# SyncE asks by a table of tiles when it may load an expert's weights, in place of a fixed distance of four tiles

## The chip, the cores and the metric

The kernel runs on one core of a Trainium2 chip. The metric is the device time of the whole program in microseconds (us), one launch, lower is better. The core's engines are TensorE (PE; its weight loads are listed as PEld), VectorE (DVE), ScalarE (ACT), GpSimd (POOL) and SyncE (SP), which computes nothing and issues DMAs. Each runs its own list of instructions in order, and they wait for each other by semaphores. A name with a "q" behind it (SPq) is the part of an engine that reads registers, branches, waits and issues.

## The reference

Two blocks on x of 8 x 256 tokens with 256 features, each an attention and a feed-forward part, all with residual additions:

```
x = x + attention0(layernorm(x), ctx, ctx)              # 16 heads, no projections
x = x + moe(layernorm(x), gate_w, w_gate, w_up, w_down) # 64 experts, top 8, F = 192
x = x + attention1(layernorm(x), ctx, Wq, Wk, Wv, Wo)   # causal
x = x + block_sparse_ffn(layernorm(x), ...)             # 16 blocks of 64, top 4
```

The change lies in moe. Each of the 2048 tokens chooses 8 of 64 experts; with g = rows of an expert times w_gate, u = rows times w_up, the expert's output is (silu(g) * u) times w_down, and a token's 8 outputs are summed with the weights of the choice:

```
topk_w, topk_ids = top_k(softmax(x @ gate_w.T), 8);  topk_w /= topk_w.sum()
g = ragged_dot(sorted_tokens, w_gate.T, group_sizes)
u = ragged_dot(sorted_tokens, w_up.T, group_sizes)
out = ragged_dot(silu(g) * u, w_down.T, group_sizes)
```

## The kernel before, in words

Stages run one behind the other: constants and preparation; attention 0, with the routing of the experts (class Route) worked into it; the expert tiles (`experts`); attention 1, with the gathering of the experts' outputs worked into it; and the last feed-forward part with the output projection.

Route writes, for each expert, a list of its tokens to DRAM (POOL, L835: 128 indirect DMAs) and then makes the tables of tiles on DVE (`make_tables`). A tile is 128 entries of one expert's list, so an expert has as many tiles as its list needs, and an expert's tiles follow each other. `k.table` has one column per tile and three rows: the expert, the buffer (the expert's number among those that have tiles, modulo WRING = 4), and 1 where the tile is its expert's first. `make_tables` computes them with the tile number on the partitions (`below`, `sums`, two halves a of 128 tiles), PE turns them onto one partition (`turned`), and DVE copies them (`line`, `line_i`). POOL meanwhile finishes the lists and gathers the tokens of each tile (`ids_raw`, L841), which DVE then converts (L1011).

`experts(nc, k, begin, end)` is called twice, for tiles 0 to 159 and for tiles 160 to 191; the second call does its work only if more than 160 tiles are in use (`needed`). In the profiled execution the lines of the stage have run for 160 tiles. Tiles are taken in rounds of R = 8, round 0 written out with constants and the others in a loop. For tile t:

- SP (`step` under `block.sync`, L1136 to L1145) reads three entries of the table into registers (`value_load`; L1136 expert, L1137 buffer, L1138 first or not), waits until `down_ready` has reached t - WRING + 1, that is until the down product of tile t - 4 is done, and issues two DMAs, w_gu (384 KB) and w_down (192 KB), each with the condition `fresh`. If the tile isn't its expert's first, no data moves and only the semaphore `w_in[j]` is raised.
- POOL gathers the 128 token rows of the tile by an indirect DMA (L1157, L1159), up to eight tiles ahead.
- PE turns the rows (L1172), multiplies them by w_gu (L1181, after it has waited for `w_in[j]`), turns the gated hidden rows of the tile before (L1191) and multiplies those by w_down (L1199), which raises `down_ready`.
- ACT copies the turned rows (L1247) and applies silu (L1253), and issues the store of the results (L1258). DVE multiplies by u (L1288), copies the turned hidden rows (L1294) and weighs the result (L1302).

`down_ready` counts down products. SP's wait for it keeps a load from overwriting a buffer that is still read; since the four buffers go around by expert and not by tile, four tiles back is sufficient for that whatever the sizes of the experts.

Of the kernel before, what the change touches and what calls it, by code (L numbers as in the profile page):

```python
# [7 lines left out]
F32 = mybir.dt.float32  # L8
BF16 = mybir.dt.bfloat16
I32 = mybir.dt.int32  # L10
ALU = mybir.AluOpType
ACT = mybir.ActivationFunctionType
AX = mybir.AxisListType

P = 128
# [21 lines left out]
START = 6  # L37
LISTS = EXPERTS * TILES
WRING = 4
IN_FLIGHT = 4  # L40

BLOCKS, TOP_B, HID = 16, 4, 1024
# [659 lines left out]
class Route:  # L702
# [8 lines left out]
    def open(self, nc, k, ctx, sem, ps):  # L711
        sb = lambda n, shape, dt: ctx.enter_context(nc.sbuf_tensor(f"rt_{n}", shape, dt))
        E = EXPERTS
        self.nc, self.k, self.ps = nc, k, ps
        self.gate = sb("gate", [P, DC, E], F32)
        self.before = sb("before", [P, P], BF16)
        self.ones = sb("ones", [P, P], BF16)
        self.list_end = sb("list_end", [P, E], F32)
        self.token = sb("token", [P, TILES], I32)
        self.tile_no = sb("tile_no", [P, 2], F32)  # L720
        self.zeros = sb("zeros", [P, LISTS], I32)
        self.stats = sb("stats", [P, 2, 6], F32)
        self.moments = sb("moments", [P, 2, 2], F32)
        self.rstd = sb("rstd", [P, 2], I32)
        self.newton = sb("newton", [P, 2], F32)
        self.rows = sb("rows", [P, 2, 2, D + E], F32)
        self.xn_t = sb("xn_t", [P, DC * SEQ], F32)
        self.logits = sb("logits", [P, 2, E], F32)
        self.others = sb("others", [P, 2, E], F32)
        self.best = sb("best", [P, 2, 8], F32)  # L730
        self.expo = sb("expo", [P, 2, E], F32)
        self.chosen = sb("chosen", [P, 2, E], F32)
        self.total = sb("total", [P, 3, 2], F32)
        self.mask = sb("mask", [P, TILES, E], BF16)
        self.earlier = sb("earlier", [P, TILES + 1, E], BF16)
        self.back = sb("back", [P, 2, E], F32)
        self.now = sb("now", [P, 2, E], F32)
        self.place = sb("place", [P, TILES, E], F32)
        self.top = sb("top", [P, 2, TOP_K], F32)
        self.idx = sb("idx", [P, TILES, TOP_K], I32)  # L740

        self.shift_g = sb("shift_g", [P, E], F32)
        self.place_g = sb("place_g", [P, TILES, E], F32)
        self.top_g = sb("top_g", [P, TILES, TOP_K], F32)
        self.count = sb("count", [P, 6, E], F32)
        self.count_i = sb("count_i", [P, E], I32)
        self.below = sb("below", [P, 2, 3, E], F32)
        self.sums = sb("sums", [P, 2, 4], F32)
        self.distinct = sb("distinct", [P, 1], F32)
        self.row = sb("row", [P, 2], F32)  # L750
        self.row_i = sb("row_i", [P, 2], I32)
        self.ids_raw = sb("ids_raw", [P, 2, P], I32)
        self.ids_f = sb("ids_f", [P, 2, P], F32)
        self.line = sb("line", [1, 3, ETABLE], F32)
        self.line_i = sb("line_i", [1, ETABLE], I32)

        self.c_in, self.zero_set, self.zeroed = sem("constants_in"), sem("zero_set"), sem("lists_zeroed")
        self.outs_zeroed = sem("outs_zeroed")
        self.own, self.none_set = sem("route_own"), sem("none_set")
        self.xn_ready, self.xn_turned, self.xn_copied, self.logits_ready = sem("xn_ready"), sem("xn_turned"), sem("xn_copied"), sem("logits_ready")  # L760
        self.shifted, self.exped, self.counted, self.ranked = sem("shifted"), sem("route_exped"), sem("counted"), sem("ranked")
        self.ranks_read, self.weights_ready, self.slots_ready = sem("ranks_read"), sem("weights_ready"), sem("slots_ready")
        self.rows_out = [sem("rows_out0"), sem("rows_out1")]
        self.scattered, self.ids_in = [k.indirect(f"scattered{q}") for q in range(IN_FLIGHT)], k.indirect("ids_in")
        self.tables, self.counts_ready = sem("tables_own"), sem("counts_ready")
        self.rows_ready, self.ids_f_ready, self.turned = sem("rows_ready"), sem("ids_f_ready"), sem("turned")
        self.constants = [(self.gate, "gate"), (self.before, "c_before"), (self.ones, "c_ones"), (self.list_end, "c_list_end"),
                          (self.token, "c_token"), (self.tile_no, "c_tile")]
# [184 lines left out]
    def make_tables(self, dve):  # L953
# [20 lines left out]
        then(nc.vector.tensor_copy(k.tiles_used[:], ends[0:1, E - 1:E]))  # L974
        then(nc.vector.tensor_scalar(some, tiles, 0.5, None, ALU.is_gt))
        then(nc.vector.tensor_reduce(distinct[:], some, AX.X, ALU.add))
        then(nc.vector.tensor_scalar(distinct[:], distinct[:], -1.0, None, ALU.add))

        for a in range(2):
            then(nc.vector.tensor_scalar(below[:, a, 0, :], ends, self.tile_no[:, a:a + 1], None, ALU.is_le))  # L980
            then(nc.vector.tensor_tensor(below[:, a, 1, :], below[:, a, 0, :], some, ALU.mult))
            then(nc.vector.tensor_tensor(below[:, a, 2, :], below[:, a, 0, :], tiles, ALU.mult))
            then(nc.vector.tensor_reduce(sums[:, a, 0:3], below[:, a], AX.X, ALU.add))
            then(nc.vector.tensor_scalar(sums[:, a, 0:1], sums[:, a, 0:1], float(E - 1), None, ALU.min))
            then(nc.vector.tensor_tensor(sums[:, a, 1:2], sums[:, a, 1:2], distinct[:], ALU.min))
            then(nc.vector.tensor_tensor(sums[:, a, 3:4], self.tile_no[:, a:a + 1], sums[:, a, 2:3], ALU.subtract))
            then(nc.vector.tensor_scalar(sums[:, a, 3:4], sums[:, a, 3:4], float(TILES - 1), None, ALU.min))
            then(nc.vector.tensor_scalar(self.row[:, a:a + 1], sums[:, a, 0:1], float(TILES), None, ALU.mult))
            nc.vector.tensor_tensor(self.row_i[:, a:a + 1], self.row[:, a:a + 1], sums[:, a, 3:4], ALU.add).then_inc(self.rows_ready, 1)

# [9 lines left out]

        dve.wait_ge(self.turned, 1)
        then(nc.vector.tensor_copy(line[:, 0:2, :].rearrange("p q n -> p (q n)"), self.ps[0:1, :]))
        then(nc.vector.memset(line[:, 2, 0:1], 1.0))
        then(nc.vector.tensor_tensor(line[:, 2, 1:ETABLE], line[:, 1, 1:ETABLE], line[:, 1, 0:ETABLE - 1], ALU.not_equal))
        then(nc.vector.tensor_copy(k.table[:, 0, :], line[:, 0, :]))
        then(nc.vector.tensor_copy(self.line_i[:], line[:, 1, :]))
        then(nc.vector.tensor_scalar(k.table[:, 1, :], self.line_i[:], WRING - 1, None, ALU.bitwise_and))
        then(nc.vector.tensor_copy(k.table[:, 2, :], line[:, 2, :]))
        dve.wait_ge(self.ids_in, 32)  # L1010
        nc.vector.tensor_copy(self.ids_f[:], self.ids_raw[:]).then_inc(self.ids_f_ready, 1)  # L1011
# [69 lines left out]
def experts(nc, k, begin, end):  # L1081
# [7 lines left out]
    with ExitStack() as ctx:  # L1089
# [32 lines left out]
        with nc.Block() as block:  # L1122
# [10 lines left out]
            def _(sp):  # L1133
                def step(i, j):
# [4 lines left out]

                    fresh = None if isinstance(i, int) and t == 0 else other > 0  # L1140

                    wait(sp, down_ready, t - WRING + 1)
                    sp.dma_start(w_gu[:, bass.ds(ring, 1)].rearrange("p a c n -> p (a c n)"),
                                 k.dram["w_gu"][bass.ds(expert, 1)].rearrange("e p c n -> (e p) (c n)"), cond=fresh).then_inc(w_in[j], 16)
                    sp.dma_start(w_down[:, bass.ds(ring, 1)].rearrange("p a c n -> p (a c n)"),  # L1145
# [20 lines left out]
            def _(pe):  # L1166
# [62 lines left out]
                        rings = step(i, j, rings, first=(isinstance(i, int) and i == j == 0), left=R - j if last else R)  # L1229

                with needed(pe):
                    turn_rows(0, 0)
                    turn_rows(0, 1)
                    steps(0)
                    with pe.Fori(1, ROUNDS - 1) as i:
                        steps(i)
                    steps(ROUNDS - 1, last=True)
                    turn_hidden(ROUNDS - 1, R - 1)
                    down(ROUNDS - 1, R - 1, buffer_of(ROUNDS - 1, R - 1))
# [43 lines left out]
            def _(dve):  # L1283
# [6 lines left out]
                def copy_hidden(i, j):  # L1290
                    t = R * i + j
                    dve.wait_ge(hidden_turned, t + 1)
                    wait(dve, down_ready, t - 1)
                    nc.vector.tensor_copy(hidden_t[:, j % 2], ps[0:FH, 4 + j % 2, 0:2 * P]).then_inc(hidden_copied, 1)  # L1294

                def weigh(i, j):
                    t = R * i + j
                    expert = dve.value_load(table[0:1, 0, bass.ds(t, 1)], min_val=0, max_val=EXPERTS - 1)
                    dve.wait_ge(down_ready, t + 1)
                    if not isinstance(i, int) or i:  # L1300
                        dve.wait_ge(out_done[j], 16 * i)
                    nc.vector.tensor_scalar(result[:, j], ps[:, 6 + j % 2, 0:D], rows[:, j, bass.ds(expert + D, 1)], None, ALU.mult).then_inc(result_ready, 1)  # L1302
# [542 lines left out]
def build(nc, dram, out):  # L1845
# [11 lines left out]
    with ExitStack() as ctx:  # L1857
# [2 lines left out]
        k.kst = sb("stacked_keys", [ROWS + MROWS, 4, HSTEP, SEQ], BF16)  # L1860
        k.ao = sb("attention_out", [P, TILES, D], F32)
        k.slot = sb("slot", [P, TILES, TOP_K], I32)
        k.table = sb("tile_table", [1, 3, ETABLE], I32)
        k.tiles_used = sb("tiles_used", [1, 1], I32)
        k.ids = sb("slot_tokens", [P, ETABLE], I32)

# [75 lines left out]
```

## Time and the profile before

| | us |
|---|---|
| median of 3 runs | 1505.9 |
| lowest and highest | 1501.64, 4754.02 |
| profiled execution, its time | 1501.42 |
| its span, first to last instruction | 1499.6 |

The mean granted TensorE clock was 0.826 of full speed in that execution. Over the whole span PE was busy for 67% and the other engines less: DVE 41%, POOL 32%, ACT 24%.
### The profile page before, as it was taken

How to read it: one execution, taken by the hardware profiler on the slowest of the kernel's cores; microseconds unless marked ns; L12 is line 12 of the kernel's file. 1: busy time of each engine (PE TensorE's matmuls, PEld its weight loads, DVE VectorE, ACT ScalarE, POOL GpSimd, SP SyncE). 2: the span in 40 equal slices, each digit the busy share in tenths (PEclk: the TensorE clock that was granted, in tenths of full speed). 3: DMA queues.
4: the chain of work that ended last, by engine and by line, in shares of the span. 5: the costliest groups of instructions: out<-in, count | busy, mean ns of one | idle time of the engine just before them, and what ended most of it. 6: DMA issues, size and time to landing. Idle time of an engine off the chain costs nothing. (4 is left out here: it accounts for less than half of the span.)

```text
span 1499.6 us, 26078 instructions
## 1 busy us (share of the span) xinstructions
PE 1007.6 (67%) x5671; PEld 650.4 (43%) x5672; DVE 617.9 (41%) x1846; ACT 361.8 (24%) x884; POOL 483.5 (32%) x641
## 2 busy tenths in 40 slices
PE   5476757640078778888888878601445658859999
PEld 4333434320045555555555555401224436636665
DVE  5467665652023333333333333322535657423220
ACT  4534343410011111111111111110023334512221
POOL 4401334455543333333333333077453320000000
PEclk9868686655589999999999999855567779969999
DMA  6766664100055454445545655235543333210000
GB/s 195 255 172 158 74 74 66 28 18 0 4 154 159 141 165 150 150 150 151 158 147 165 176 164 157 86 98 139 139 112 109 101 99 92 52 69 11 15 14 18
DMA packets 102128, 164.36 MB, mean 110 GB/s; under 512 B 20352, under 2 KB 70400, under 8 KB 101808
## 3 DMA queue, kind: packets, MB, share of 16 engines
q1 hardware_dynamic: 61040, 99.39, 24.4%
q0 software_dynamic: 17984, 43.21, 10.8%
q10 hardware_dynamic: 23040, 20.98, 4.2%
q8 instruction: 30, 0.49, 0.2%
q14 instruction: 34, 0.28, 0.1%
HBM read 174.72 MB, written 45.15 MB: 147 GB/s over the span
## 5 line engine op out<-in xcount | busy, mean ns | idle before, releaser
L1181 PE MATMUL ex_ps<-ex_w_gu,ex_rows_t 128*128 x640 | 278.5, 518 | 89.8 <-DMA ex_w_down<-in_w_down_dram 70.8
L1159 POOL DMA_INDIRECT ex_rows<-moe_rows,ex_idx x160 | 155.5, 972 | 129.1 <-POOL ex_idx L1157 117.7
L835 POOL DMA_INDIRECT expert_lists<-rt_token,rt_idx x128 | 124.4, 972 | 203.9 <-DMA expert_lists<-rt_token,rt_idx 110.4
L647 ACT ACTIVATE a_probs<-a_ps 128x512 f32<-128x512 f32 (+1 forms) x256 | 133.8, 540 | 206.3 <-remote 67.1
L1199 PE MATMUL ex_ps<-ex_w_down,ex_hidden_t 96*128 x640 | 169.6, 388 | 1.0 <-DVE ex_hidden_t L1294 1.0
L492 PE MATMUL a_ps<-stacked_keys,a_qst 96*128 96x256 bf16 (+1 forms) x512 | 119.6, 307 | 73.8 <-DMA stacked_keys<-k_stack 30.4
L1181 PEld LDWEIGHTS ex_ps<-ex_w_gu,ex_rows_t 128*128 128x128 f32 x640 | 108.4, 198 | 121.7 <-issue 116.4
L509 PE MATMUL a_ps<-a_qst,stacked_keys 98*128 98x256 bf16 (+1 forms) x512 | 116.5, 301 | 65.9 <-issue 30.3
L1253 ACT ACTIVATE ex_act_g<-ex_ps 128x192 f32<-128x192 f32 x160 | 52.8, 330 | 440.2 <-PE ex_ps L1181 412.3
L1391 POOL DMA_INDIRECT cb_gathered<-expert_outs,cb_idx x128 | 122.1, 954 | 45.0 <-issue 40.9
L1294 DVE COPY ex_hidden_t<-ex_ps 96x256 f32<-96x256 f32 x160 | 67.3, 420 | 142.7 <-PE ex_ps L1191 126.2
L1302 DVE TENSOR_SCALAR ex_result<-ex_ps,ex_rows 128x256 f32<-128x256 f32 x160 | 77.4, 484 | 96.0 <-PE ex_ps L1199 85.8
L1199 PEld LDWEIGHTS ex_ps<-ex_w_down,ex_hidden_t 96*128 96x128 f32 x640 | 110.9, 194 | 12.4 <-issue 2.3
L588 DVE TENSOR_REDUCE a_negmax<-a_ps 128x2 f32<-128x512 f32 x128 | 85.8, 688 | 63.4 <-PE a_ps L492 52.1
L585 DVE TENSOR_REDUCE a_blockmax<-a_ps 128x3 f32<-128x384 f32 x128 | 70.2, 554 | 96.7 <-remote 49.2
L1288 DVE TENSOR_TENSOR ex_hidden<-ex_act_g,ex_ps 128x192 f32<-128x192 f32 x160 | 56.7, 354 | 115.0 <-ACT ex_act_g L1253 110.9
L1157 POOL COPY ex_idx<-slot_tokens 128x1 int32 (+1 forms) x160 | 29.3, 183 | 224.6 <-DVE ex_result L1302 216.7
L492 PEld LDWEIGHTS a_ps<-stacked_keys,a_qst 96*128 96x128 bf16 x512 | 51.2, 112 | 115.9 <-issue 43.3
L509 PEld LDWEIGHTS a_ps<-a_qst,stacked_keys 98*128 98x128 bf16 x512 | 54.0, 111 | 96.0 <-issue 54.8
L1649 POOL TENSOR_TENSOR x<-x,ff_b 128x256 f32 x16 | 11.5, 747 | 226.0 <-DVE ff_xn L1805 226.0
L1247 ACT COPY ex_rows_t<-ex_ps 128x256 f32<-128x256 f32 x160 | 58.8, 368 | 92.8 <-PE ex_ps L1172 91.5
L532 PE MATMUL a_ps<-a_probs,a_v_aug 128*32 128x256 f32 (+1 forms) x1024 | 79.4, 439 | 0.0
(200 smaller groups left out, 1405.0 us busy)
## 6 DMA issues: line engine op xcount, KB each, us to landing
ex_w_gu<-in_w_gu_dram SPq DMA_DIRECT2D x160, 384.0 KB
ex_w_down<-in_w_down_dram SPq DMA_DIRECT2D x160, 192.0 KB
expert_outs<-ex_result ACTq DMA_DIRECT2D x160, 128.0 KB
k_stack<-split_parts SPq DMA_DIRECT2D x16, 384.0 KB, 2.6
a_qst<-q_stack SPq DMA_DIRECT2D x32, 192.0 KB
stacked_keys<-k_stack SPq DMA_DIRECT2D x32, 192.0 KB
a_qst<-q_stack SPq DMA_DIRECT2D x32, 128.0 KB
stacked_keys<-k_stack SPq DMA_DIRECT2D x32, 128.0 KB
```

The lines of the kernel that those rows point to most:

```text
L492: last = pe.matmul(bank[:, at:at + keys], qst[0:ROWS, u, s, j * P:(j + 1) * P], kst[0:ROWS, u, s, 0:keys], start=True, stop=True)
L509: last = pe.matmul(bank[:, at:at + SEQ - first], kst[:, u, s, j * P:(j + 1) * P], qst[:, u, s, first:SEQ], start=True, stop=True)
L532: last = pe.matmul(outs_dq[VW * r:VW * (r + 1), first:SEQ], v_aug[:, b_par, j, s, :], probs[:, 4 * g + r, j * SEQ:j * SEQ + SEQ - first], ...
L585: nc.vector.tensor_reduce(blockmax[:, u % 2, s, :], ps[:, QK_BANKS[s % 3], 0:cols].rearrange("p (b n) -> p b n", n=P), AX.X, ALU.max, nega ...
L588: nc.vector.tensor_reduce(negmax[:, u % 2, :, s], ps[:, QK_BANKS[s % 3], :].rearrange("p (j n) -> p j n", j=2), AX.X, ALU.max, negate=True ...
L647: nc.scalar.activation(probs[:, s, 0:cols], ps[:, 2 + s % 2, 0:cols], ACT.Exp, scale=scale).then_inc(exped, 1)
L835: nc.gpsimd.indirect_dma_start(k.lists, bass.IndirectOffsetOnAxis(ap=self.idx[:, t, s:s + 1], axis=0), self.token[:, t:t + 1], None).then_ ...
L1159: nc.gpsimd.indirect_dma_start(rows[:, j, :], None, k.xn.rearrange("t p d -> (t p) d"), bass.IndirectOffsetOnAxis(ap=idx[:, j:j + 1], axis ...
L1181: last = pe.matmul(ps[:, 2 + j % 2, 0:2 * FF], rows_t[:, j % 2, c * P:(c + 1) * P], w_gu[:, bass.ds(ring, 1), c, :].rearrange("p a n -> p ...
L1199: last = pe.matmul(ps[:, 6 + j % 2, 0:D], hidden_t[:, j % 2, c * P:(c + 1) * P], w_down[:, bass.ds(ring, 1), c, :].rearrange("p a n -> p ( ...
L1302: nc.vector.tensor_scalar(result[:, j], ps[:, 6 + j % 2, 0:D], rows[:, j, bass.ds(expert + D, 1)], None, ALU.mult).then_inc(result_ready, 1)
L1391: nc.gpsimd.indirect_dma_start(self.gathered[:, u, j, s, :], None, k.outs.rearrange("t p d -> (t p) d"), bass.IndirectOffsetOnAxis(ap=self ...
```

## The change

SP's wait takes its count from a fourth row of the table. For a tile of expert number d (among those with tiles) it holds the number of tiles of the experts up to number d - 4, the last user of the buffer, or the tile's number minus 7 if that is more (so that SP is at most eight tiles ahead, the number of the semaphores `w_in`), and one is added. PE raises `down_ready` by one at its start, so that the count is never zero, and DVE's waits for `down_ready` and the fixed distance of the second call are one higher. `make_tables` computes the new row: a running count of the experts with tiles (`kinds`), for each half four operations for the count and one that packs it with the expert's number into one value, and for the line an integer copy, a shift and a mask that take them apart.

```diff
+LOADS_AHEAD = 8
...
             then(nc.vector.tensor_reduce(distinct[:], some, AX.X, ALU.add))
+            then(nc.vector.tensor_tensor_scan(self.kinds[:], one, some, 0.0, ALU.mult, ALU.add))
...
         for a in range(2):
...
+            then(nc.vector.tensor_scalar(below[:, a, 3, :], self.kinds[:], float(WRING - 1), sums[:, a, 1:2], ALU.add, ALU.is_le))
+            then(nc.vector.tensor_tensor(below[:, a, 3, :], below[:, a, 3, :], tiles, ALU.mult))
+            then(nc.vector.tensor_reduce(sums[:, a, 4:5], below[:, a, 3, :], AX.X, ALU.add))
+            then(nc.vector.scalar_tensor_tensor(sums[:, a, 4:5], self.tile_no[:, a:a + 1], float(1 - LOADS_AHEAD), sums[:, a, 4:5], ALU.add, ALU.max))
+            then(nc.vector.tensor_scalar(sums[:, a, 0:1], sums[:, a, 0:1], 256.0, sums[:, a, 4:5], ALU.mult, ALU.add))
...
+        then(nc.vector.tensor_copy(self.line_i[:, 0, :], line[:, 0, :]))
...
-        then(nc.vector.tensor_copy(k.table[:, 0, :], line[:, 0, :]))
-        then(nc.vector.tensor_copy(self.line_i[:], line[:, 1, :]))
-        then(nc.vector.tensor_scalar(k.table[:, 1, :], self.line_i[:], WRING - 1, None, ALU.bitwise_and))
+        then(nc.vector.tensor_scalar(k.table[:, 0, :], self.line_i[:, 0, :], 8, None, ALU.logical_shift_right))
+        then(nc.vector.tensor_scalar(self.line_i[:, 0, :], self.line_i[:, 0, :], 255, None, ALU.bitwise_and))
+        then(nc.vector.tensor_scalar(k.table[:, 3, :], self.line_i[:, 0, :], 1.0, None, ALU.add))
+        then(nc.vector.tensor_copy(self.line_i[:, 1, :], line[:, 1, :]))
+        then(nc.vector.tensor_scalar(k.table[:, 1, :], self.line_i[:, 1, :], WRING - 1, None, ALU.bitwise_and))
...
                     fresh = None if isinstance(i, int) and t == 0 else other > 0
-                    wait(sp, down_ready, t - WRING + 1)
+                    if begin == 0:
+                        used = sp.value_load(table[0:1, 3, bass.ds(t, 1)], min_val=1, max_val=ETILES)
+                        sp.wait_ge(down_ready, used)
+                    else:
+                        wait(sp, down_ready, t - WRING + 2)
...
                 with needed(pe):
+                    pe.sem_inc(down_ready, 1)
...
-                    wait(dve, down_ready, t - 1)
+                    wait(dve, down_ready, t)
...
-                    dve.wait_ge(down_ready, t + 1)
+                    dve.wait_ge(down_ready, t + 2)
...
-        k.table = sb("tile_table", [1, 3, ETABLE], I32)
+        k.table = sb("tile_table", [1, 4, ETABLE], I32)
```

## Rows read from the trace of the kernel before

**Rows 1.** Windows by stage; the columns stand in the first line.

```profile
core 0: us, PE busy (x) PEld busy (x) DVE busy (x) ACT busy (x) POOL busy (x), PEclk, DMA share, GB/s
0.00:300.00 300.00, 195.07 (x1293) 114.04 (x1295) 182.23 (x579) 126.31 (x261) 100.11 (x98) 0.78 0.55 128
300.00:413.00 113.00, 20.17 (x107) 11.00 (x105) 27.98 (x131) 7.06 (x15) 61.50 (x64) 0.50 0.04 8
421.00:960.00 539.00, 449.19 (x1904) 297.56 (x1905) 199.08 (x475) 98.23 (x319) 180.46 (x313) 0.96 0.51 155
```

**Rows 2.** Waits of PE from 430 to 960: total us, times, longest.

```profile
PE ex_ps L1181 <- DMA ex_w_down<-in_w_down_dram: 70.8, 43, 3.4
PE ex_ps L1181 <- issue: 18.6, 18, 1.6
```

**Rows 3.** Waits of SP, the line of the loads.

```profile
SPq L1143 <- PE ex_ps L1199: 5.6, 9, 1.4
```

**Rows 4.** SP by source line: ns min/median/max, first and last start.

```profile
L1137 SPq TENSOR_LOAD <-tile_table x160: 5/267/520, 414.3 to 955.4; - x160
L1138 SPq TENSOR_LOAD <-tile_table x160: 3/263/524, 414.8 to 956.1; - x160
L1143 SPq DMA_DIRECT2D ex_w_gu<-in_w_gu_dram x160: 4/97/673, 415.6 to 957.0; - x160
L1145 SPq DMA_DIRECT2D ex_w_down<-in_w_down_dram x160: 5/93/549, 416.2 to 957.5; - x160
```

**Rows 5.** Timeline of PE, 429 to 435: the starts of three tiles.

```profile
429.61 0.81 PE L1181 MATMUL ex_ps<-ex_w_gu,ex_rows_t 128*128 x2
...
432.21 0.81 PE L1181 MATMUL ex_ps<-ex_w_gu,ex_rows_t 128*128 x2
...
434.81 0.81 PE L1181 MATMUL ex_ps<-ex_w_gu,ex_rows_t 128*128 x2
```

**Rows 6.** Timeline of PE, 465 to 475, and L1181 by source.

```profile
465.27 1.64 PE L1181 MATMUL ex_ps<-ex_w_gu,ex_rows_t 128*128 x2 [2.55 <-DMA ex_w_down<-in_w_down_dram]
...
469.47 0.81 PE L1181 MATMUL ex_ps<-ex_w_gu,ex_rows_t 128*128 x2
...
L1181 PE MATMUL ex_ps<-ex_w_gu,ex_rows_t x640: 484/488/1004, 421.4 to 960.4; 128*128 x160
```

**Rows 7.** SP by source line within 444 to 447 us, one tile.

```profile
L1136 SPq FUSED_REGOPS  x2: 51/110/169, 444.4 to 444.8; - x2
L1136 SPq TENSOR_LOAD <-tile_table x1: 275/275/275, 444.5 to 444.5; - x1
L1137 SPq FUSED_REGOPS  x2: 51/102/153, 445.0 to 445.4; - x2
L1137 SPq TENSOR_LOAD <-tile_table x1: 267/267/267, 445.1 to 445.1; - x1
L1137 SPq SEQ_ASSERT  x1: 18/18/18, 445.6 to 445.6; - x1
L1138 SPq FUSED_REGOPS  x2: 51/99/147, 445.7 to 446.1; - x2
L1138 SPq TENSOR_LOAD <-tile_table x1: 263/263/263, 445.8 to 445.8; - x1
L1138 SPq SEQ_ASSERT  x1: 16/16/16, 446.4 to 446.4; - x1
L1143 SPq FUSED_REGOPS  x2: 48/114/179, 446.5 to 446.7; - x2
```

**Rows 8.** SP's computed counts of the helper `wait`, L55.

```profile
L55 SPq ALU_OP  x57: 13/37/282, 439.5 to 940.7; - x57
```

**Rows 9.** Timeline ahead of the stage: POOL's gather of ids, DVE's conversion.

```profile
404.10 0.97 POOL L841 DMA_INDIRECT rt_ids_raw<-expert_lists,rt_row_i  x1 [3.62 <-DMA expert_lists<-rt_token,rt_idx]
405.38 0.96 POOL L841 DMA_INDIRECT rt_ids_raw<-expert_lists,rt_row_i  x1 [0.30 <-issue]
408.48 0.29 DVE L1011 CAST rt_ids_f<-rt_ids_raw 128x256 f32<-128x256 int32 x1 [62.08 <-DMA rt_ids_raw<-expert_lists,rt_row_i]
```

More of the change, by code:

```diff
@@ L746, in open @@
         self.count_i = sb("count_i", [P, E], I32)
-        self.below = sb("below", [P, 2, 3, E], F32)
-        self.sums = sb("sums", [P, 2, 4], F32)
+        self.below = sb("below", [P, 2, 4, E], F32)
+        self.sums = sb("sums", [P, 2, 5], F32)
         self.distinct = sb("distinct", [P, 1], F32)
@@ L754, in open @@
         self.line = sb("line", [1, 3, ETABLE], F32)
-        self.line_i = sb("line_i", [1, ETABLE], I32)
+        self.line_i = sb("line_i", [1, 2, ETABLE], I32)
+        self.kinds = sb("kinds", [P, E], F32)
         self.c_in, self.zero_set, self.zeroed = sem("constants_in"), sem("zero_set"), sem("lists_zeroed")
@@ L982, in make_tables @@
             then(nc.vector.tensor_tensor(below[:, a, 2, :], below[:, a, 0, :], tiles, ALU.mult))
-            then(nc.vector.tensor_reduce(sums[:, a, 0:3], below[:, a], AX.X, ALU.add))
+            then(nc.vector.tensor_reduce(sums[:, a, 0:3], below[:, a, 0:3], AX.X, ALU.add))
             then(nc.vector.tensor_scalar(sums[:, a, 0:1], sums[:, a, 0:1], float(E - 1), None, ALU.min))
```

## The prediction

> **What bounds the kernel now.** I began with the windows by stage [rows 1]. The change touches one stage, the expert tiles from 421 to 960 us: 539 of the 1499.6 us, at a granted TensorE clock of 0.96. No engine's column is full there (PE 449 of 539 us), so the next question is what PE waits for. The waits of PE [rows 2] say: 70.8 us in 43 waits for the landing of ex_w_down, and only 18.6 us at its own issue. Read by itself, this is a stage whose weights come too late, and loading them earlier looks like the cure.
>
> The other end of that wait must be read before that is believed: what kept SyncE from issuing earlier? The waits of SP [rows 3] answer it. At L1143 SP waited for the down products of PE (the wait that the change loosens) 5.6 us in total, nine times, at most 1.4 us. So in most of the 160 tiles the buffer was already free when SP came to ask. Outside those nine, SP isn't four tiles ahead; it is late by its own work. The sources of SP show that work [rows 4]: it issues the first w_gu load at 415.6 and the 160th at 957.0, that is 541.4 us for 159 steps, 3.41 us a tile. PE's own pace, where nothing holds it, is read from the starts of consecutive tiles [rows 5]: 429.61, 432.21, 434.81, which is 2.60 us a tile, or 416 us for 160. The stage lasts as long as SP's list of instructions and not as long as PE's, and PE's last w_gu product starts at 960.4, 3 us after SP's last issue [rows 4, 6].
>
> Where do 3.41 us go when the two DMA issues take 97 and 93 ns at the median [rows 4]? Each tile reads three entries of the table into registers, and each read is two FUSED_REGOPS, a TENSOR_LOAD of some 265 ns and a SEQ_ASSERT [rows 7]. In the step at 444 to 447 us the reads of L1136, L1137, L1138 begin at 444.4, 445.0 and 445.7 and the work of L1143 at 446.5 [rows 7]. Three reads are 2.1 of that step's time. The rows of SP list no idle time inside them.
>
> The Trainium skill, in "Perfetto Trace Analysis", section "What DMA-bound means", gives as the sign of a bound DMA issuer a sequencer track that is solid with DMA slices. Here that sign fails: the DMA slices are about a tenth of SP's step, and it is solid with register loads. By that sign SP would be passed over.
>
> **The change, part by part.**
>
> SP, new read (one per tile). Where the address is computed at run time, a read costs (445.7 - 444.4) / 2 = 0.65 us of SP's time [rows 7]; its parts 51 + 267 + 153 + 18 ns are 0.49, and the rest is the pause after each of four instructions. In round 0 the addresses are constants and there is no first FUSED_REGOPS; L1137 and L1138 begin at 414.3 and 414.8 [rows 4], so 0.55 by these rounded rows and the parts without the 51 ns. 152 x 0.65 + 8 x 0.55 = 103 us. Nothing lies beside it: SP runs its instructions one behind the other, and the new read stands ahead of the wait and of both loads. The bounds: 0.50 us, if every new read were as short as the first spacing, gives 80; 0.8 us, the longest spacing in rows 7 (445.7 to 446.5), gives 128. I take 0.65 because the reads of the loop are the like of the new one, and the third spacing holds a pause ahead of its SEQ_ASSERT (446.4) that the first two lack.
>
> SP, the computed count. `wait` computed t - 3 in an instruction of its own for three tiles of a round: 57 ALU_OPs of 37 ns [rows 8]. They go: 2 us, at most 4 with the pause behind them. The wait itself rides on the next instruction before and after, and I cost a register count as I do the computed one, at nothing; as a separate instruction of the ALU_OP's length it would be 160 x 0.04 = 6 us more, inside the bounds above.
>
> SP, the looser wait. It can give back no more than the 5.6 us that SP waited [rows 3]. Who gains from a lead of eight tiles? Only a queue that gets ahead. SP needs 3.41 now and about 4.0 then, PE 2.60, so SP will hardly reach the old limit of four, let alone eight. The new count is never stricter than the old one (a buffer's former expert ended at least four tiles back), so no new wait comes, and nothing is queued behind one. The rank of the loads, their bytes and their queue stay.
>
> PE, DVE inside the stage: one semaphore increment at the start, and counts one higher for DVE's waits. They concern work that is not late. Nothing.
>
> DVE, the tables: one scan, ten short operations for the two halves and three for the line, each behind a semaphore. DVE sits idle for 62.08 us before it may convert the ids at 408.48, since the ids come from POOL's scatters and gather [rows 9]. Fourteen operations with their waits at 1 us each (the conversion there takes 0.29) would be 14 us, under 62. Nothing on the path. Without that cover it would be those 14 us at most.
>
> PE must wait longer per tile for the weights, which is the place where the time shows: its waits grow by what SP's step grows. The clock is the second-order term. After a stall of 2.55 us PE ran its next tile at half speed, and that tile took 469.47 - 465.27 = 4.20 us [rows 6]. More stall means more of those. In stages where PE is busy 65% of the time the clock stood at 0.78 [rows 1]; after the change PE has 2.6 us of work in a step of 4.0, the same share. At 0.78, 44% of the tiles would take 4.20 and the others 2.60, a mean of 3.3, still under SP's 4.0. So the clock falls, and the end doesn't feel it.
>
> **The sum.** 103 (read) - 2 (ALU_OPs) - 6 (waits) = +95 us on SP's list and so on the stage. The profiled execution took 1501.42 us around a span of 1499.6; the middle one of the three runs is 1505.9 and the lowest 1501.64, so the profiled one stands at their low end. 1501.4 + 95 = 1596.4 us, +6.3% on that execution, +6.0% on 1505.9. Where the stall goes: PE waits some 95 us more for the loads, and the granted clock of the stage drops from 0.96 toward 0.8.
>
> **The rivals.**
>
> Faster (A). The loads land early and PE keeps its own pace. The stage is then 160 x 2.60 = 416 in place of 539 us: 1501 - 123 = 1378. For it: the 70.8 us in rows 2. It decides if SP in truth waited for buffers for most of its time, which [rows 3] deny with 5.6 us, or if a read of the table costs SP nothing. The rule behind it is in the Trainium skill, "DMA: Bandwidth & Descriptors", "Rules for kernel authors": issue a DMA early and wait for it late, so that its fixed cost overlaps. The rule would want it; the trace shows that this issuer has no earlier time to issue at.
>
> Not slower (B). The fourth read overlaps the third, so that it adds at most 0.2 us: 160 x 0.2 - 6 = +26, so 1527, within 2%. It decides if a TENSOR_LOAD's 265 ns are latency which the next read can run under. Against it: in rows 7 each read starts only after the last one's SEQ_ASSERT.
>
> Slower by more (C). The stalls hold TensorE at half clock in the whole stage. A tile then costs 4.20 us and PE is the bound: 160 x 4.20 = 672 against 539, so 1634. It decides from a mean tile of 4.0 us upward, which is a granted clock under about 0.57. In rows 1 the clock was 0.50 only where PE was busy less than a fifth of the time.
>
> That the change does not do what it says: SP really does ask by the new count, but its lead stays under four tiles. That is no rival, since it is the forecast.
>
> **How the numbers follow.** The forecast (slower by a read per tile) 88%, C 5%, B 4%, A 3%. Within the forecast the bounds of the read give 80 - 4 - 6 = +70, 1571, and 128 - 2 - 6 = +120, 1621. The cases outside hold 12% between them, so the range is 1571 to 1621 and needn't reach them. About 2% (30 us) is what a measurement of this kernel tells from no change; with it, slower 0.93, same 0.04, faster 0.03.
>
> **What would show it.** In the profile after: a fourth group of TENSOR_LOAD x160 on SP at the new read; SP's first to last w_gu issue about 637 us; SP's wait for the down products near zero; the waits of PE for ex_w_down risen, not gone; the stage's clock near 0.8; DVE still idle for tens of us ahead of the conversion of the ids. The prediction is wrong if SP's waits of L1143 hide time that no row shows, or if SP's step grows by much less than 0.6 us.

## The result and the profile after

| | us | ratio to the kernel before |
|---|---|---|
| before, median | 1508.03 | |
| after, median of 4 runs (1589.94 to 1600.35) | 1598.56 | 1.0604, 95% interval 1.0542 to 1.0666 |
| predicted | 1596.0 (1571 to 1621) | |

The change makes the kernel 6% slower. One of the four runs of before took 4754.02 us and is left out of the ratio, which comes from means; this ratio and those below can differ by up to 0.4% from the quotient of the medians. The profiled execution of after took 1596.96 us, with a span of 1595.1, which is 95.5 us more than before's 1499.6.

The windows of the kernel after, the stage of the expert tiles alone (columns: start:end and length in us, busy time of PE, PEld, DVE, ACT, POOL, then the granted clock, the DMA share and GB/s):

```profile
421.00:1055.00 634.00, 484.90 (x1900) 316.69 (x1900) 198.39 (x473) 99.98 (x319) 184.18 (x317) 0.90 0.44 133
```

It answers to the third row of [rows 1]: the same work of every engine, in 634 us in place of 539. DMA moved 133 GB/s where it had moved 155: the same bytes, spread over more time. That no collision of transfers stands behind the loss is for the first experiment to show.

The waits of PE and of SP in that stage of the kernel after (total us, times, longest):

```profile
PE ex_ps L1196 <- DMA ex_w_down<-in_w_down_dram: 131.6, 54, 5.7
PE ex_ps L1196 <- issue: 12.8, 11, 1.6
...
SPq L1158 <- PE ex_ps L1214: 0.9, 4, 0.2
```

PE's wait for the weights, which the looser wait was to shorten, went from 70.8 us [rows 2] to 131.6, and its longest from 3.4 to 5.7. SP's wait for the down products went from 5.6 us [rows 3] to 0.9. Both moved together: SP hardly ever stands, and PE stands longer. An issuer that waits for nothing and is still late is late by its own list.

That list, by source line (count, ns min/median/max, first and last start), the new read at L1154:

```profile
L1149 SPq TENSOR_LOAD <-tile_table x160: 3/263/661, 420.0 to 1054.4; - x160
...
L1154 SPq FUSED_REGOPS  x312: 3/109/370, 420.8 to 1055.3; - x156
L1154 SPq TENSOR_LOAD <-tile_table x160: 3/263/754, 420.5 to 1055.0; - x160
L1154 SPq SEQ_ASSERT  x160: 3/18/348, 421.0 to 1055.5; - x160
...
L1158 SPq DMA_DIRECT2D ex_w_gu<-in_w_gu_dram x160: 4/93/399, 421.3 to 1056.0; - x160
```

From the first w_gu issue to the 160th, 421.3 to 1056.0, is 634.7 us; before it was 541.4 [rows 4]. That is +93.3 us for 160 reads. The same four parts as in [rows 7] are there once more per tile.

What the longer step does to PE is seen in its timeline after, at three consecutive tiles:

```profile
500.86 0.81 PE L1196 MATMUL ex_ps<-ex_w_gu,ex_rows_t 128*128 x2
...
507.80 1.64 PE L1196 MATMUL ex_ps<-ex_w_gu,ex_rows_t 128*128 x2 [4.18 <-DMA ex_w_down<-in_w_down_dram]
...
511.37 1.80 PE L1214 MATMUL ex_ps<-ex_w_down,ex_hidden_t 96*128 x4
513.00 0.81 PE L1196 MATMUL ex_ps<-ex_w_gu,ex_rows_t 128*128 x2
```

PE stands for 4.18 us, then runs its next two matmuls in 1.64 us in place of 0.81, at half clock, and it is still at half clock at the end of that tile (1.80 us for four matmuls, 1.03 at full clock), which takes 5.20 us. Before, such a pair stood in [rows 6]. The slow tiles don't lengthen the stage: SP was held up by PE for 0.9 us in all of it, and PE's last w_gu matmul starts at 1057.9, 1.9 us after SP's last issue. A tile of 5.20 is longer than SP's step (634.7 / 159 = 3.99 us), but there are few, and PE makes up for them in tiles of 2.60.

The table operations stayed hidden. After, DVE's conversion of the ids shows:

```profile
413.60 0.29 DVE L1022 CAST rt_ids_f<-rt_ids_raw 128x256 f32<-128x256 int32 x1 [58.19 <-DMA rt_ids_raw<-expert_lists,rt_row_i]
```

It stood idle for 58.19 us against 62.08 in [rows 9]: some 4 us of the cover used, 58 left. The conversion itself came 5.1 us later than before; so did the scatters ahead of it. The table operations are not the cause: among the experiments below, the kernel with the tables alone issues its first w_gu load at 412.8, and the one with eight buffers and the old tables at 423.3, so shifts of this size come without the change. Added up: the stage's start +5.7 (421.3 against 415.6), SP's list +93.3, the rest of the span -3.5 (539.1 against 542.6 after SP's last issue), together +95.5.

### The profile page after: what moved, and what is told of

Its sections match the earlier page's. It is cut to its first block and busy times, and to the rows that moved or that the text cites. A ratio compares the mean times of both kernels' runs of the same rounds, so it can differ in the third digit from the quotient of the medians.

```text
span 1595.1 us, 26688 instructions
## 1 busy us (share of the span) xinstructions
PE 1033.5 (65%) x5671; PEld 666.8 (42%) x5672; DVE 621.7 (39%) x1860; ACT 363.2 (23%) x884; POOL 484.9 (30%) x641
## 5 line engine op out<-in xcount | busy, mean ns | idle before, releaser
L1196 PE MATMUL ex_ps<-ex_w_gu,ex_rows_t 128*128 x640 | 298.9, 552 | 145.2 <-DMA ex_w_down<-in_w_down_dram 131.6
L1196 PEld LDWEIGHTS ex_ps<-ex_w_gu,ex_rows_t 128*128 128x128 f32 x640 | 114.9, 211 | 181.1 <-issue 175.1
L1214 PE MATMUL ex_ps<-ex_w_down,ex_hidden_t 96*128 x640 | 180.2, 407 | 1.1 <-DVE ex_hidden_t L1310 1.1
L1214 PEld LDWEIGHTS ex_ps<-ex_w_down,ex_hidden_t 96*128 96x128 f32 x640 | 118.7, 207 | 14.2 <-issue 2.4
L1187 PEld LDWEIGHTS ex_ps<-ident,ex_rows 128*128 128x128 f32 x320 | 49.4, 155 | 71.3 <-issue 42.8
```

Source lines behind the costliest of these rows:

```text
L1196: last = pe.matmul(ps[:, 2 + j % 2, 0:2 * FF], rows_t[:, j % 2, c * P:(c + 1) * P], w_gu[:, bass.ds(ring, 1), c, :].rearrange("p a n -> p ...
L1214: last = pe.matmul(ps[:, 6 + j % 2, 0:D], hidden_t[:, j % 2, c * P:(c + 1) * P], w_down[:, bass.ds(ring, 1), c, :].rearrange("p a n -> p ( ...
```

## The experiments

The theory: **SyncE's own list of instructions paces the stage**, and each read of the table into a register is on the path at its full length. The rivals: **the looser wait does the harm** (earlier loads collide with gathers and stores); **the tables or the counts do**; and, from the other side, **the loads do come too late for want of lookahead**, and the new read only covers that gain. The first six ran on one chip, the two with a branch on a second and the last four on a third; ratios are to runs of the kernel before on the same chip.

**One read alone, the wait as it was.** The edit on the kernel before, with a fourth row in the table:

```diff
                     other = sp.value_load(table[0:1, 2, bass.ds(t, 1)], min_val=0, max_val=1)
+                    sp.value_load(table[0:1, 3, bass.ds(t, 1)], min_val=0, max_val=1)
```

> The kernel before with one more read of the table per tile on SyncE, from a fourth row, whose value nobody uses; the fixed distance of four tiles stays. If SyncE's list of instructions paces the stage, the time is that of the changed kernel plus at most the few us of waiting that the looser wait gave back: +93 to +103 us on the kernel before, 1597 to 1608, a ratio of 1.060 to 1.068. Rival: the changed kernel is slower because the looser wait starts loads that collide with gathers and stores; then the read by itself costs nothing, a ratio of 1.00.

Measured: 1596.35 us, ratio 1.0651 (1.0582 to 1.0720), the time of the changed kernel. The waits of PE and SP and SP's w_gu issues in that run:

```profile
PE ex_ps L1183 <- DMA ex_w_down<-in_w_down_dram: 132.4, 50, 5.6
...
SPq L1145 <- PE ex_ps L1201: 0.5, 2, 0.3
...
L1145 SPq DMA_DIRECT2D ex_w_gu<-in_w_gu_dram x160: 4/93/545, 420.7 to 1056.6; - x160
```

132.4 us of waiting for ex_w_down against after's 131.6, with the old distance of four tiles. The whole loss is there without the looser wait, so the wait and the loads it moves have no part in it.

**Two reads.** The same with two unused reads.

> The kernel before with two unused reads per tile in place of one. If each read is on the path at its full 0.65 us, the time rises twice as much as with one: +190 to +205 us, 1698 to 1713, a ratio of 1.126 to 1.136. If something else saturates (PE at half clock, say) the second read costs more or less than the first.

Measured: 1695.14 us, ratio 1.1286 (1.1206 to 1.1366): the ratio as expected, the time 3 us under the range that I gave.

```profile
PE ex_ps L1185 <- DMA ex_w_down<-in_w_down_dram: 205.8, 66, 6.1
...
L1147 SPq DMA_DIRECT2D ex_w_gu<-in_w_gu_dram x160: 13/97/635, 425.4 to 1160.4; - x160
```

SP's first to last issue is 635.9 us with one read more and 735.0 with two: 99.1 us for the second, 0.62 us for each of 160. Nothing saturates up to two more: one read, one price.

**The tables alone.** The changed kernel, but SP waits by the fixed distance and doesn't read the fourth row:

```diff
-                    if begin == 0:
-                        used = sp.value_load(table[0:1, 3, bass.ds(t, 1)], min_val=1, max_val=ETILES)
-                        sp.wait_ge(down_ready, used)
-                    else:
-                        wait(sp, down_ready, t - WRING + 2)
+                    wait(sp, down_ready, t - WRING + 2)
```

> The changed kernel with all its table operations, the raised semaphore and the longer table, but SyncE waits by the fixed distance of four tiles and does not read the fourth row. Theory of the paced list: the time of the kernel before, within 5 us (the table operations lie in an idle stretch of VectorE of some 60 us), ratio 0.997 to 1.003. Rival: the tables or the higher counts carry part of the +95 us, a ratio of 1.01 or more.

Measured: 1502.28 us, ratio 0.9997 (0.9962 to 1.0032). The fourteen DVE operations, the raised semaphore and the higher counts cost nothing that ten runs can tell: the interval allows some 5 us either way, against the 95.

**The lookahead alone.** Eight buffers and a fixed distance of eight, no new read:

```diff
-WRING = 4
+WRING = 8
```

> The kernel before with eight weight buffers and so a fixed distance of eight tiles (WRING 8): the looser wait without any new read. Theory of the paced list: it can return only the 5.6 us that SyncE waited, a ratio of 0.996 to 1.000. Rival that weights come too late for want of lookahead: the 70.8 us of waits shrink, ratio 0.95 or less. Rival that earlier loads collide with other transfers: slower, a ratio above 1.01.

Measured: 1503.72 us, ratio 1.0007 (0.9970 to 1.0045).

```profile
SPq L1143 <- PE ex_ps L1199: 0.7, 4, 0.2
...
PE ex_ps L1181 <- DMA ex_w_down<-in_w_down_dram: 75.3, 45, 3.5
```

This is the change's idea without its price. SP's wait fell from 5.6 to 0.7 us, and PE's wait for the weights stayed at 75.3 us. Lookahead that the issuer has no time to use is worth nothing here, and costs nothing either.

**One word for three reads.** If SP paces the stage, fewer reads must make it shorter. DVE packs expert, buffer and "first" into one word of the table; SP reads once and takes it apart:

```diff
-                    expert = sp.value_load(table[0:1, 0, bass.ds(t, 1)], min_val=0, max_val=EXPERTS - 1)
-                    ring = sp.value_load(table[0:1, 1, bass.ds(t, 1)], min_val=0, max_val=WRING - 1)
-                    other = sp.value_load(table[0:1, 2, bass.ds(t, 1)], min_val=0, max_val=1)
+                    word = sp.value_load(table[0:1, 3, bass.ds(t, 1)], min_val=0, max_val=2 ** 18 - 1)
+                    expert = sp.snap(sp.to_reg((word >> 3) & (EXPERTS - 1)), min_val=0, max_val=EXPERTS - 1)
+                    ring = sp.snap(sp.to_reg((word >> 1) & (WRING - 1)), min_val=0, max_val=WRING - 1)
+                    other = sp.snap(sp.to_reg(word & 1), min_val=0, max_val=1)
```

> The kernel before, fixed distance of four tiles, but the three entries of a tile (expert, buffer, first or not) are packed into one word of the table; SyncE reads once and takes them apart with shifts and masks. Two reads less are 1.3 us, four or five register operations more about 0.3, so its step falls from 3.41 to some 2.4 us, under PE's 2.60. The bound then passes to PE and the latency of the loads: the stage takes 416 to 440 us in place of 539, 1385 to 1410 us in all, a ratio of 0.92 to 0.94, the waits of SyncE for the down products rise to tens of us. If SyncE's list did not pace the stage, a ratio of 1.00.

Measured: 1428.44 us, ratio 0.9506 (0.9465 to 0.9547), 5% faster than the kernel before, but 18 to 43 us above what I expected.

**The same with the table's count**, packed into the word as well (`used = word >> 9`), on the changed kernel:

> The changed kernel with all four entries in one word: the table's count decides the wait, and SyncE reads once. SyncE's step is some 2.5 us. Beside the kernel with one word and the fixed distance it tells what the lookahead is worth where SyncE no longer paces. With a distance of four tiles a load has about 3 x 2.60 = 7.8 us from its release to its use, and it takes about 6 from the issue to PE's start, so I expect little from more lookahead: equal to that kernel within 1%, 1380 to 1410 us. Rival: the lookahead does what it was written for once SyncE has time, and this one is faster than that kernel by over 1.5%.

Measured: 1417.66 us, ratio 0.9435 (0.9376 to 0.9493). Now the changed kernel's wait seems to pay its way; this time too is above my range, by 8 us. The waits of both, the fixed distance first:

```profile
SPq L1148 <- PE ex_ps L1204: 21.6, 33, 1.3
...
PE ex_ps L1186 <- issue: 27.0, 25, 1.6
PE ex_ps L1186 <- DMA ex_w_down<-in_w_down_dram: 11.5, 13, 1.6
```

```profile
SPq L1166 <- PE ex_ps L1222: 0.5, 2, 0.3
...
PE ex_ps L1204 <- issue: 26.4, 20, 1.6
...
PE ex_ps L1204 <- DMA ex_w_down<-in_w_down_dram: 3.0, 3, 1.4
```

With time to spare SP did run into the distance of four (21.6 us), and the table removed that. The difference, 0.7% in the ratios, is inside the 1% that I had called equal, and the two ratios' intervals overlap; all four runs of the one lie above all four of the other (from 1426.31 against up to 1424.82), and the next pair repeats the comparison with more runs. PE's waits for the weights are down to 3.0 us, from 70.8.

Where the size was off: SP's step with one word is (876.1 - 423.8) / 159 = 2.84 us, and not 2.5, by these rows of the kernel with one word and the table's count:

```profile
L1154 SPq TENSOR_LOAD <-tile_table x160: 12/268/786, 422.1 to 874.5; - x160
L1155 SPq ALU_OP  x320: 3/37/528, 423.0 to 875.2; - x160
L1155 SPq FUSED_REGOPS  x160: 3/64/602, 423.1 to 875.2; - x160
L1156 SPq ALU_OP  x160: 2/33/685, 423.3 to 875.4; - x160
L1156 SPq MOVE  x160: 3/34/277, 423.3 to 875.4; - x160
L1157 SPq ALU_OP  x159: 3/33/690, 426.3 to 875.5; - x159
L1157 SPq FUSED_REGOPS  x159: 5/116/706, 426.3 to 875.6; - x159
L1166 SPq DMA_DIRECT2D ex_w_gu<-in_w_gu_dram x160: 4/97/657, 423.8 to 876.1; - x160
```

Taking the word apart is seven instructions of 33 to 116 ns, 354 ns, and each has a pause behind it. With the pauses it costs about what one of the three reads costs that it saves: three reads at 0.62 are 1.86 us, and SP's step fell by 3.99 - 2.84 = 1.15, so some 0.7 went back. SP waited only 0.5 us here, so at 2.84 us a step it still paced the stage on this chip.

**A branch around the empty loads.** With this branch SP issues each load 64 times (the count in its trace) and not 160, so 64 tiles are their expert's first; for the other 96 SP read expert and buffer and issued two conditional loads that move nothing. Here it reads "first" first:

```diff
+                    other = sp.value_load(table[0:1, 2, bass.ds(t, 1)], min_val=0, max_val=1)
+                    with sp.If(other > 0):
+                        load()          # the other reads, the wait, the two loads without a condition
+                    with sp.Else():
+                        wait(sp, down_ready, t - LOADS_AHEAD + 2)
+                        sp.sem_inc(w_in[j], 32)
```

On the changed kernel, with the table's count:

> The changed kernel with a branch: SyncE reads first whether the tile is its expert's first; only then it reads the other three entries and issues the two loads, and else it waits until the tile eight back is done and raises the semaphore of the loads by a plain increment. 64 tiles of 160 take about 4.2 us on SyncE, 96 about 1.2 us, a mean of 2.4, under PE's 2.60. With the table's count SyncE may run ahead over a large expert's tiles. The stage falls toward 416 to 430 us, 1385 to 1400 us in all, a ratio of 0.92 to 0.935, PE's waits for the loads under 15 us and SyncE waiting for tens of us.

Measured: 1344.09 us where the kernel before took 1423.64 on that chip, ratio 0.9430 (0.9401 to 0.9459), less of a gain than the 0.92 to 0.935 that I had given. The same branch on the kernel before, three reads and the fixed distance of four (in its other arm too):

> The kernel before with the same branch, three reads for a first tile, fixed distance of four tiles. SyncE's mean is 2.2 us a tile, but its work comes in lumps of 3.6 us and the distance of four caps what it may run ahead. If lookahead is of use once the issuer has time, this one is slower than the one with the table in spite of a read less, by 5 to 20 us (some 1400 to 1415 us); if lookahead is worth nothing, it is equal or faster.

Measured: 1353.18 us, ratio 0.9492 (0.9460 to 0.9523). The absolute times that I gave suit the first chip and not this one (below). Between the two kernels the table's count is worth 9 us, 0.6%, within the 5 to 20 that I had given, although it costs one more read for each of 64 tiles. The intervals just part, and all six runs of the one lie above all six of the other (from 1347.91 against up to 1345.75). The traces agree: PE's first to last tile is 459.6 us with the fixed distance and 446.4 with the table, and only with the fixed distance does PE still wait for weights:

```profile
PE ex_ps L1188 <- DMA ex_w_down<-in_w_down_dram: 9.6, 11, 1.4
```

The fixed-distance kernel limits both arms of the branch to four tiles and the other kernel to the table's count and to eight, so the 9 us are those of the whole lookahead. SP's waits, the fixed distance first and then the table:

```profile
SPq L1153 <- PE ex_ps L1206: 107.5, 89, 5.5
...
SPq L1140 <- PE ex_ps L1206: 32.8, 54, 2.2
```

```profile
SPq L1168 <- PE ex_ps L1221: 52.7, 38, 3.3
...
SPq L1155 <- PE ex_ps L1221: 23.9, 16, 2.5
```

SP now waits 77 us and more of the stage, where it waited 5.6. It has ceased to be the bound. But the stage did not fall to the 416 us that I had given for a free PE. The waits of PE, and its timeline at the end of a round, in the kernel with branch and table:

```profile
PE ex_ps L1203 <- issue: 26.5, 20, 1.6
...
472.46 1.03 PE L1221 MATMUL ex_ps<-ex_w_down,ex_hidden_t 96*128 x4
475.12 0.91 PE L1203 MATMUL ex_ps<-ex_w_gu,ex_rows_t 128*128 x2 [1.64 <-issue]
```

PE waits for no load of weights any more. It stands 20 times at its own issue, once per round of eight tiles, where its loop branches back and it reads two buffer numbers before the first matmul. Such a tile takes 4.1 us and not 2.60. 159 x 2.60 + 19 x 1.5 = 442 us, and the trace has 446 from the first tile to the last.

**The last group: PE's loop over two rounds.** Four kernels on one chip, to settle what bounds now.

```diff
-                    with pe.Fori(1, ROUNDS - 1) as i:
-                        steps(i)
+                    with pe.Fori(0, (ROUNDS - 2) // 2) as h:
+                        rings = steps(2 * h + 1, carry=True)
+                        steps(2 * h + 2, rings=rings)
```

(`carry` reads the next round's first buffer number inside the last tile of a round, as for every other tile.)

> The kernel before once more, unchanged, for its trace on this chip: SyncE's first to last load issue 541 us within 8 us, its step near 3.4 us, PE's waits for ex_w_down near 70 us, whatever the length of the other stages here.

> The kernel with one word per tile and the table's count, again, beside the one with the branch on the same chip. Its stage took 451 us from PE's first to last tile and the branch kernel's 446, so I expect it 3 to 8 us slower than that one: both are now at PE's own pace.

> The kernel with the branch and the table's count, again. PE's first to last tile 446 us: 159 steps of 2.60 plus 1.5 us at each of 19 ends of a round.

> The branch kernel with PE's loop written out for two rounds, so that PE ends a loop pass (branch, and two reads of the buffer number with nothing queued) 10 times in place of 19. If PE's own list is now the bound, each end saved gives 1.5 us: 14 us less, 1% (a stage of 432 us). If something else is the bound, no change.

| kernel | us | ratio to before | PE, first to last tile |
|---|---|---|---|
| before (one profiled run; the ratios are to 7 runs, median 1423.74) | 1433.0 | | 531.9 |
| one word, table's count | 1341.18 | 0.9401 (0.9346 to 0.9455) | 446.4 |
| branch, table's count | 1342.03 | 0.9434 (0.9374 to 0.9493) | 446.8 |
| branch, table's count, PE in pairs of rounds | 1328.55 | 0.9332 (0.9272 to 0.9392) | 432.5 |

The last column is the distance between the first w_gu matmul of tile 0 and of tile 159. One word and the branch come out equal; I had expected the word to be 3 to 8 us behind, from two traces of different chips (451.4 against 446.4); on one chip the gap is gone. Both are at the same floor, PE's. SP's list of the one-word kernel is shorter here than it was on the first chip: 438.3 us from first to last issue (421.3 to 859.6), of which SP waited 18.9 where it had waited 0.5:

```profile
SPq L1166 <- PE ex_ps L1222: 18.9, 15, 2.4
```

That leaves 2.64 us a step without waiting, against 2.84 on the first chip, so SP no longer paces it. Why SP was quicker here wasn't looked for. The kernel before did here what was expected: 535.7 us from SP's first to last issue and 68.6 us of PE's waits for ex_w_down. The pairs take 14.3 us off it, the forecast 14, and PE's stands at its own issue show where (the branch kernel first, then the pairs):

```profile
PE ex_ps L1203 <- issue: 26.6, 20, 1.6
```

```profile
PE ex_ps L1203 <- issue: 14.7, 11, 1.6
```

20 stands became 11. In the medians it is 13.5 us; the two intervals overlap, and it is mainly the traces that show it, though the runs agree: the slowest of the pairs, 1336.28, is just under the fastest of the other, 1336.62. This kernel, 6.7% under the kernel before and so about 12% under the changed one (0.9332 / 1.0604 = 0.88, of two chips), is the fastest that the runs point to.

## Why the prediction was right

**SP as the bound: right.** SP's waits of 5.6 us against PE's of 70.8 [rows 2, 3] carried the argument. Four runs bear it out from different sides: the read alone gives the whole loss, two give it twice, lookahead alone gives nothing, fewer reads give 5%.

**The new read, 0.65 us and 103 us: right, a little high.** The second read cost 99.1 us, 0.62 each. The first cost 94.5 on the list (635.9 against 541.4) and took the waits of some 5 us away with it, which is the same 99 to 100.

**The waits given back, 5.6 us: right in size,** 4.7 (5.6 to 0.9). **The 57 ALU_OPs, 2 us,** are too small to be seen by themselves. The sum was +95; SP's list grew by 93.3, and the span by 95.5. That the span came within half a us is luck: the read was put 4 us too high, and +5.7 ahead of the stage and -3.5 behind it, neither of which was forecast, went into the 95.5.

**The tables at nothing: right,** by the tables alone (0.9997) and by the 58.19 us that DVE still stood idle.

**PE's waits: the direction right, the size not.** I wrote that they would grow by the 95 us. The waits named in the trace grew from 89.4 to 144.8, by 55, and PE's busy time took a part of the rest: 484.9 against 449.2 us, since its matmuls ran longer at half clock.

**The clock, 0.8: wrong.** It stood at 0.90. I had taken PE's share of work as 2.6 of 4.0 us, 65%, and looked for a stage with that share in the busy column. The busy column of this stage says 76% (484.9 of 634), because tiles that run at half clock stay in it longer (484.9 us are 3.03 a tile, not 2.60): two different shares were laid side by side. That two stages of one share have one clock was assumed as well, and no run tests it. The "44% of the tiles" was a slip besides: a clock of 0.78 puts 44% of the time, not of the tiles, at half clock. The term was second-order and no part of the sum.

**Rival C (half clock throughout, 1634) and rival B (1527)** did not come, but C's price was too low. Its 4.20 us is a tile [rows 6] that was back at full clock before it ended; its last four matmuls in the trace before:

```profile
468.61 1.03 PE L1199 MATMUL ex_ps<-ex_w_down,ex_hidden_t 96*128 x4
```

A tile at half clock to its end takes 5.20 us, as the trace after shows. Half clock throughout would have been 160 x 5.20 = 832 us of stage and an estimated 1794 in all, and PE would have become the bound once (4.0 - 2.6) / (5.2 - 2.6) = 54% of the tiles were slow, where 4.20 a tile gives 88%. The case was nearer than its 5% made it look. The forecast's "still under SP's 4.0" leaned on the lower figure; it held because PE's busy time came to 3.03 us a tile. **Rival A's price was wrong** though its case didn't come either: 160 x 2.60 = 416 us as PE's own pace left out the ends of rounds. The rows chosen for the pace, three tiles inside one round [rows 5], could not show them. PE's floor is 446, so the most that any cure of SP could bring was about 92 us (537.8 - 446) and not 123. The same mistake stands behind my too low times for the one-word kernels, together with the 0.35 us and pauses of taking the word apart.

**The step I'd put more carefully:** "it will hardly reach the old limit" held for this kernel and says nothing on the idea. Once SP has time, the table's count is worth some 9 us by the pair with the branch.

## What to carry to other kernels

When an engine waits for a DMA, ask first what the issuing engine waited for. If it waited for nothing, an earlier permission to issue can't help; count the instructions in its step, reads of registers and conditional DMAs that move nothing included, since none of them shows as busy. In this kernel one read of a value at a computed address, 0.62 us, cost SyncE more than the instruction that issues a DMA (0.35 us, and under 0.1 where no data moves), so adding one to save a wait pays only where the wait is longer than that per turn. And take the pace of a loop over a whole pass of it, with its end, not over a few turns in the middle.

## What the runs showed of the hardware that I had not expected

- A read of a table entry into a register of SyncE (two register instructions, a TENSOR_LOAD of 263 ns, a bounds check) cost 0.62 us of its time and did not overlap with the next one: the second extra read cost 99.1 us over 160 tiles, and the first 94.5 plus the 5 us of waiting that it swallowed.
- A register instruction of SyncE (ALU_OP) is recorded with 33 to 37 ns, but in the one-word kernel's trace on the third chip 62 to 72 ns (median) pass from its start to the next instruction's, so unpacking by shifts and masks isn't free.
- A DMA issue is recorded much longer where data moves. In the branch kernel, whose 64 loads all move data, the shortest w_gu issue is 351 ns; the median of 97 ns over 160 [rows 4] is mostly that of loads that move nothing.

```profile
L1155 SPq DMA_DIRECT2D ex_w_gu<-in_w_gu_dram x64: 351/355/394, 417.9 to 846.1; - x64
```

- The same program, the kernel before, took about 1503 us on one chip and 1424 on two others. In the profiled executions of 1501.42 and 1433.0 us the stage of the expert tiles was alike (PE's first to last tile 537.8 and 531.9 us); the difference lies behind it, 540 against 466 us from the last tile to the end. I didn't look for its cause, and it stays open; it is why ratios and not times are compared here.
- The end of a loop pass costs PE a stand of 1.4 to 1.6 us in this kernel (26.6 us in 20 stands); nine fewer took 14.3 us off, 1% of the whole.
